# A decoder layer on one core: the order of work of four engines in the loop body, written anew

## The reference, cut to what matters

```python
# x, ctx: (64, 128, 512) float32
x = x + mamba(layernorm(x))                    # inner width 1024, 16 states a channel
x = x + xattn(layernorm(x), ctx)               # 8 heads of 16, tokens 512, band of +-64
x = x + moe(layernorm(x))                      # 8 experts of 16, the best 2 of them

def mamba(x):
    h_in, gate = split(x @ in_proj_w.T)
    u = silu(causal_conv4(h_in) + conv_b)
    ts, Bm, Cm = split(u @ x_proj_w.T)         # 128, 16, 16
    dt = softplus(ts @ dt_proj_w.T + dt_proj_b)
    h[t] = exp(dt[t] * A) * h[t-1] + dt[t] * u[t] * Bm[t]     # for each channel and state
    y = (sum over states of h * Cm + D * u) * silu(gate)
    return y @ out_proj_w.T

def xattn(x, ctx):                             # a sequence is (128 channels, 512 tokens)
    q, k, v = split(x.T @ w_in.T + b_in)
    a = softmax(where(|i - j| <= 64, q k / 4, -inf))
    return w_ct.T @ (relu((a v @ w_out.T + b_out).T) * ctx) + b_ct
```

## Time and profile before

| | |
|---|---|
| median of 3 runs | 5236.79 us (5234.45 to 5239.43) |
| span of the profiled execution | 5221.2 us, 15.6 below the median |
| mean granted TensorE clock | 0.976 |
| one iteration in the loop | 154.7 us |
| share of the span busy | PE 90%, DVE 88%, ACT 84%, POOL 83% |

### The profile page before, as it was taken

The page is one execution under the profiler, slowest core; times in us unless marked ns, Lnnn a source line. Parts: engine busy times, 40 slices in busy tenths (PEclk is TensorE's granted clock), DMA queues, the critical chain, the costliest instruction groups (busy, mean ns, idle before and its releaser), DMA issues. The chain is left out here.

```text
span 5221.2 us, 141020 instructions
## 1 busy us (share of the span) xinstructions
PE 4699.5 (90%) x51012; PEld 3370.9 (65%) x51012; DVE 4617.0 (88%) x6307; ACT 4384.6 (84%) x9314; POOL 4311.4 (83%) x3466
## 2 busy tenths in 40 slices
PE   4789999999999999999999999999999999998976
PEld 3566666666666666666666666666666666666653
DVE  2889999999999999999999999999999999998961
ACT  3788889888898888889988898988889888888862
POOL 2888888888898888888888888888889888888860
PEclk8899999999999999999999999999999999999986
DMA  3202222212222211222221222221222221122200
GB/s 118 74 29 79 70 76 78 78 41 74 72 71 78 78 58 56 72 74 78 74 78 36 78 69 78 78 78 41 73 72 70 78 78 57 57 72 71 66 13 7
DMA packets 114706, 350.31 MB, mean 67 GB/s; under 512 B 13056, under 2 KB 14848, under 8 KB 113920
## 3 DMA queue, kind: packets, MB, share of 16 engines
q1 hardware_dynamic: 114048, 341.51, 20.2%
HBM read 323.64 MB, written 17.83 MB: 65 GB/s over the span
## 5 line engine op out<-in xcount | busy, mean ns | idle before, releaser
L304 POOL TENSOR_TENSOR ring<-du,bc 128x512 f32<-128x512 f32 x2048 | 2594.2, 1284 | 622.0 <-PE ps L1128 408.5
L472 ACT ACTIVATE ps<-delta,a_neg 128x254 f32<-128x254 f32 x4096 | 1767.9, 467 | 38.3 <-DVE ring L1508 25.5
L313 POOL TENSOR_TENSOR ring<-ring,bc 128x512 f32<-128x512 f32 x1280 | 1703.3, 1337 | 109.1 <-DVE ring L1508 106.7
L1508 DVE TENSOR_TENSOR_SCAN ring<-ps,ring 128x512 f32<-128x512 f32 x1280 | 1549.1, 1215 | 102.6 <-ACT ps L472 83.6
L1128 PE MATMUL ps<-ident,ring 128*128 128x128 f32 x8192 | 1096.3, 278 | 46.8 <-POOL ring L313 41.6
L1128 PEld LDWEIGHTS ps<-ident,ring 128*128 128x128 f32 x8192 | 926.1, 142 | 253.2 <-issue 169.7
L1508 DVE TENSOR_TENSOR_SCAN ps<-ps,ring 128x512 f32<-128x512 f32 x768 | 933.6, 1216 | 116.5 <-ACT ps L472 109.7
L1492 DVE TENSOR_TENSOR ring<-ps,bc 128x512 f32<-128x512 f32 x768 | 527.7, 687 | 15.7
L627 ACT ACTIVATE probs_mem<-ps 128x768 f32<-128x768 f32 (+1 forms) x512 | 445.6, 911 | 105.7 <-PE ps L1072 99.5
L1196 PE MATMUL ps<-w_in,xt_a 128*128 128x256 f32 x2048 | 474.3, 386 | 16.1 <-DVE hc L1623 8.1
L1176 PE MATMUL ps<-xt_a,w_in 128*128 128x256 f32 x2048 | 472.0, 384 | 7.6 <-DVE hc L1623 4.1
(11 more groups left out here) (144 smaller groups left out, 6915.0 us busy)
## 6 DMA issues: line engine op xcount, KB each, us to landing
w_in<-in_w_in SPq DMA_DIRECT2D x256, 512.0 KB, 3.7
bc<-bc_rows SPq DMA_DIRECT2D x256, 512.0 KB, 5.1
x_new<-in_x SPq DMA_DIRECT2D x32, 512.0 KB, 7.4
x_res<-in_x SPq DMA_DIRECT2D x32, 512.0 KB, 6.7
enc<-in_ctx SPq DMA_DIRECT2D x64, 256.0 KB, 3.1
out<-x_att SPq DMA_DIRECT2D x32, 512.0 KB, 2.8
w_outp<-in_w_outp SPq DMA_DIRECT2D x1, 2048.0 KB, 8.1
bc_rows<-bc_sb SPq DMA_DIRECT2D x32, 32.0 KB, 1.5
```

Source lines behind the costliest of these rows:

```text
L304: nc.gpsimd.tensor_tensor(ring[:, s % RING, :].rearrange("p (n t) -> p n t", n=2), du[:, q % 2, (ic % 2) * NT:(ic % 2 + 1) * NT].rearrange ...
L313: nc.gpsimd.tensor_tensor(ring[:, s % RING, :], ring[:, s % RING, :], bc[:, s % RS, 2:4, :].rearrange("p a t -> p (a t)"), ALU.mult).then_ ...
L472: nc.scalar.activation(ps[:, s % DAR, (n % 2) * NT:(n % 2 + 1) * NT].rearrange("p (b t) -> p b t", b=GB)[:, :, 1:T], delta[:, ic, :].rearr ...
L1508: nc.vector.tensor_tensor_scan(state, ps[:, s % DAR, :], ring[:, s % RING, :], 0.0, ALU.mult, ALU.add).then_inc(h_done, 1)
```

## The change

In the `iteration` functions of GpSimd, ScalarE, TensorE and VectorE the calls are put in another order. Every engine keeps the same calls, each with its waits, buffers and semaphores; the bodies of the helpers don't change. Some of what moves: on VectorE `shift` e,0 stands ahead of scan 0, and the soft steps of pair 0 stand in a row ahead of scan 62, three of pair 1 in a row behind scan 63; on GpSimd `rstd` e moves behind times_b 2; on ScalarE `soft_exp` 3, `skip_term`s, `attention_x` 1 and the group of `u_silu` and `gate_silu` move; on TensorE the scores s of the attention, h_in, gate_in and y_sum are interleaved otherwise. The diff, cut to the parts that the text speaks of:

```diff
@@ -317,121 +317,122 @@
             def iteration(g, cur, nxt, p1, p2):
                 if cur:
                     times_b(g, 0)
+                    times_b(g, 1)
                 if p1:
                     times_c(g - 1, 62)
+                if cur:
+                    times_b(g, 2)
                 if p2:
                     rstd("e", g - 2, 0, 2)
                 if cur:
-                    times_b(g, 1)
-                    times_b(g, 2)
-                    times_c(g, 0)
                     times_b(g, 3)
                     times_b(g, 4)
                     times_b(g, 5)
+                    times_c(g, 0)
                     times_b(g, 6)
                     times_b(g, 7)
                     times_c(g, 2)
+                    times_b(g, 8)
+                    times_b(g, 9)
...
+                if nxt:
+                    squares("a", g + 1, 0)
+                if p1:
                     variance("t", g - 1, 0)
-                if cur:
-                    soft_exp(g, 2)
-                    decays(g, 8)
-                    decays(g, 9)
...
+                    variance("t", g - 1, 1)
+                if cur:
                     decays(g, 16)
-                if nxt:
-                    x_norm(j, 1)
+                    soft_exp(g, 2)
+                    skip_term(g, 2)
+                if nxt:
+                    x_copy(j, 0)
...
+                    attention_x(g - 1, 1)
+                if cur:
+                    y_back(g, 0)
                     decays(g, 19)
-                    y_back(g, 0)
                     decays(g, 20)
-                    skip_term(g, 3)
+                    soft_exp(g, 3)
                     decays(g, 21)
-                    decays(g, 22)
...
-                if cur:
+                    attention(g, p2, 1, "qk", 3)
+                if cur:
+                    y_back(g, 2)
                     decays(g, 33)
-                    soft_exp(g, 3)
-                    soft_one(g, 3)
-                    skip_term(g, 5)
+                if p1:
...
-                if cur:
-                    decays(g, 44)
+                    skip_term(g, 7)
                 if p1:
                     attention(g, p2, 1, "exp", 0)
-                if cur:
-                    decays(g, 45)
-                    skip_term(g, 7)
-                if p1:
                     attention(g, p2, 1, "exp", 1)
-                    variance("e", g - 1, 0)
                 if cur:
                     decays(g, 46)
                     decays(g, 47)
-                if nxt:
-                    tap3(j, 3)
                 if p1:
                     attention(g, p2, 1, "exp", 2)
                     attention(g, p2, 1, "exp", 3)
+                if nxt:
+                    u_silu(j, 2)
+                if p1:
+                    attention(g, p2, 1, "o", 0)
+                if cur:
+                    y_back(g, 4)
+                if nxt:
+                    gate_silu(j, 0)
+                    u_silu(j, 3)
                 if cur:
                     decays(g, 48)
-                if nxt:
-                    gate_silu(j, 0)
-                if p1:
-                    attention(g, p2, 1, "o", 0)
-                if nxt:
-                    u_silu(j, 2)
-                    u_silu(j, 3)
-                if cur:
-                    y_back(g, 4)
                     decays(g, 49)
                 if p1:
                     attention(g, p2, 1, "exp", 4)
...
-                if nxt:
-                    skip_term(j, 0)
                 if p1:
                     attention(g, p2, 1, "o", 1)
+                if nxt:
+                    step_size(j, 0)
                 if cur:
                     decays(g, 57)
+                if p1:
+                    attention(g, p2, 1, "wide")
+                if nxt:
+                    soft_exp(j, 0)
+                    step_size(j, 1)
+                if cur:
                     decays(g, 58)
-                if p1:
-                    attention(g, p2, 1, "wide")
-                if nxt:
-                    step_size(j, 0)
+                if nxt:
+                    soft_one(j, 0)
                 if cur:
                     decays(g, 59)
                 if nxt:
-                    soft_exp(j, 0)
+                    step_size(j, 2)
...
-                if p2:
                     experts_up(g - 2)
                 if cur:
                     y_sum(g, 9)
+                    y_sum(g, 11)
                 if p1:
                     attention(g, p2, 0, "s", 0)
                 if nxt:
                     transposed_x(g, 0, cur, p1)
+                if cur:
+                    y_sum(g, 13)
                 if p1:
                     attention(g, p2, 0, "s", 1)
-                if cur:
-                    y_sum(g, 11)
-                if p1:
-                    attention(g, p2, 0, "s", 2)
-                if cur:
-                    y_sum(g, 13)
                 if nxt:
                     transposed_x(g, 1, cur, p1)
-                if p1:
-                    attention(g, p2, 0, "s", 3)
                 if cur:
                     y_sum(g, 15)
                     y_turn(g, 0, nxt)
                 if p1:
+                    attention(g, p2, 0, "s", 2)
+                    attention(g, p2, 0, "s", 3)
+                if nxt:
+                    h_in(j, 0, cur)
+                if p1:
                     attention(g, p2, 0, "shift")
-                if nxt:
-                    h_in(j, 0, cur)
-                if p1:
                     attention(g, p2, 0, "st", 0)
...
                 if p1:
                     attention(g, p2, 1, "s", 1)
                 if cur:
                     y_sum(g, 33)
+                    y_sum(g, 35)
+                    y_turn(g, 3, nxt)
+                    y_sum(g, 37)
                 if p1:
                     attention(g, p2, 1, "s", 2)
-                if cur:
-                    y_sum(g, 35)
-                    y_sum(g, 37)
+                if nxt:
+                    gate_in(j, 1, cur)
+                if cur:
+                    y_sum(g, 39)
                 if p1:
                     attention(g, p2, 1, "s", 3)
-                if cur:
-                    y_sum(g, 39)
-                    y_turn(g, 3, nxt)
+                if nxt:
+                    h_in(j, 3, cur)
                 if p1:
                     attention(g, p2, 1, "shift")
-                if nxt:
-                    gate_in(j, 1, cur)
+                if cur:
+                    y_sum(g, 41)
                 if p1:
                     attention(g, p2, 1, "st", 0)
-                if cur:
-                    y_sum(g, 41)
-                if nxt:
-                    h_in(j, 3, cur)
-                if p1:
                     attention(g, p2, 1, "st", 1)
                 if cur:
                     y_sum(g, 43)
                 if p1:
                     attention(g, p2, 1, "av", 0)
...
@@ -1626,57 +1621,58 @@
 
             def iteration(g, cur, nxt, p1, p2):
                 j = g + 1
-                if cur:
-                    scan(g, 0)
                 if p2:
                     shift("e", g - 2, 0)
+                if cur:
+                    scan(g, 0)
+                    soft_step(4, g, 1)
+                if p2:
                     shift("e", g - 2, 1)
-                if p1:
-                    y_step(g - 1, 7)
                 if cur:
                     scan(g, 1)
                     times_c(g, 1)
                     scan(g, 2)
+                if p1:
+                    y_step(g - 1, 7)
+                if cur:
                     scan(g, 3)
                     scan(g, 4)
                     times_c(g, 4)
-                    soft_step(4, g, 1)
                     scan(g, 5)
...
+                if cur:
+                    scan(g, 37)
                     times_c(g, 36)
-                    scan(g, 37)
-                if p1:
-                    attention(g, 1, "max", 0)
-                if cur:
+                    soft_step(2, g, 3)
                     y_step(g, 3)
+                if nxt:
+                    conv(j, 4)
+                    conv(j, 5)
+                if p1:
+                    attention(g, 1, "max", 1)
+                if cur:
                     scan(g, 38)
-                    soft_step(1, g, 3)
-                if p1:
-                    attention(g, 1, "max", 1)
-                if nxt:
...
@@ -1811,40 +1807,37 @@
                     scan(g, 54)
                     scan(g, 55)
                     times_c(g, 55)
+                if p1:
+                    attention(g, 1, "rden")
+                if cur:
                     scan(g, 56)
-                if p1:
-                    attention(g, 1, "rden")
-                if cur:
                     scan(g, 57)
                     times_c(g, 57)
+                if p1:
+                    attention(g, 1, "on")
+                if cur:
                     scan(g, 58)
-                if p1:
```

(20 more changed lines are left out.)

## The result

| | before | changed |
|---|---|---|
| median, us | 5238.1 (4 runs) | 5367.1 (5365.6 to 5370.2, 4 runs) |
| ratio | 1 | 1.0248, 95% interval 1.0234 to 1.0263 |
| span of the profiled execution, us | 5221.2 | 5365.7 |
| VectorE busy, us | 4617.0 | 4783.9 |
| one iteration in the middle, us | 154.7 | 160.4 |

The change makes the kernel 2.5% slower, 129 us. The forecast was 0.4% slower, 5258 us, with a range that ended at 5325.

What follows compares the result with a forecast made beforehand. No engine alone was the bound; VectorE's row of work was taken as the iteration's clock. Waits -2.8 and soft steps +3.5 gave +0.7 us an iteration, 22 us over 31: 5258 us, range 5165 to 5325.

Steps and rivals of the forecast that it cites:

- What costs nothing: Whole program: same instructions, 13 table loads an iteration as before, DMA triggers barely moved, first and last stages at nothing.
- the prediction's own mechanism: A VectorE instruction with two SBUF inputs and a GpSimd instruction reading SBUF contend; the second blocks until the first ends.
- Soft steps, +3.5 us: VectorE's softplus steps, put in rows under a busy GpSimd, take 3.5 us more of VectorE's time an iteration.
- The seven steps at the end: Steps 1 to 4 of pair 0 and 1 to 3 of pair 1: 5.3 and 4.55 us, 2.95 more than before.
- The nine others: The iteration's other soft steps, some newly finding GpSimd idle and some no more: +0.5 us together.
- Waits, 8.5 to 5.7 us: VectorE's waits for other engines over an iteration, summed place by place: a gain of 2.8 us.
- Head of VectorE, 0.5 us: Start of VectorE's iteration: shift e,0 ahead of scan 0 waits 0.5 us for GpSimd's later rstd e.
- (a): Rival: VectorE's soft steps don't pay, as GpSimd is held or idles; only waits count, 5107 to 5150 us; chance 0.30.
- (b): Rival: no net change, waits and soft steps cancel within 0.3 us an iteration, 5227 to 5247 us; chance 0.18.
- (c): Rival: the chain through the attention of sequence 1 becomes the bound, 2.5 us more an iteration, 5335 us; chance 0.10.
- The marks given for a right forecast: End soft steps near 1.8 us, decays' wait 5.5 to about 3, rden over 1 us, rstd e waited for at the head.

Runs made afterwards that it cites:

- after_psum: Changed kernel with the router's exponentials, indices and one comparison mask in PSUM instead of SBUF; 5244.4 us, 1.0010.
- after_tail: Changed kernel with the seven soft steps at the end of VectorE's iteration back where they stood before; 5428.3 us, 1.0375.
- psum_fill01: after_psum with TensorE's scores 2 of sequence 0 ahead of y_sum 15 and y_turn 0, and y_sum 41 between st 0 and st 1 of sequence 1; 5300.2 us, 1.0122.

## Why the prediction was wrong, point by point

- **What costs nothing.** This is the step that failed. It counted table loads and DMA triggers and took the router, whose place on VectorE hardly changes, at nothing, though the prediction's own mechanism applies to it: five instructions with two SBUF inputs beside GpSimd. They cost 3.6 us an iteration, and through the gates 1.6 us of waits and a clock at half for 7 us. after_psum removes exactly this and with it 123 of the 129 us of the whole; of the 5.8 us by which the iteration in the middle grew it takes away 3.4 (157.0 us), and the rest is in the next two terms. The start and the end of the program, also put at nothing, were not nothing either: the first iteration with a scan got 6.6 us shorter and the part behind the last scan 0 4.2.
- **Soft steps, +3.5 us.** The mechanism was right and the size too large: 2.0. The seven steps at the end were put at 5.3 + 4.55 us; the timeline of the changed kernel has 0.97 + 1.65 + 1.66 + 0.69 = 5.0 and 1.13 + 1.64 + 1.64 = 4.4, against 6.9 before. The nine others were to cost 0.5 more and cost 0.5 less. A held step takes 1.64 to 1.66 us rather than the 1.8 assumed: by the traces it ends 0.55 us behind the product that holds it, which is the own pass of 0.56 assumed, so that only 1.1 us of the product were left and not the whole 1.28.
- **Waits, 8.5 to 5.7 us.** They are 9.1. Those forecast came about: 3.1 us at scan 48 (2.7), 1.7 at rden 1 (1.5), 0.4 at addq of sequence 1 (0.6), 0.4 at maximum 0.0 (0.2). On top came 1.6 for the experts, from the router, 0.7 at addq of sequence 0, 1.0 at scan 29 and 0.3 at rden 0, which I had not seen. In after_psum, without the router, the sum is 9.7 in an iteration with two stretches at half clock and 6.9 in one at full clock. So the order does take waits away, 1.6 us of the 2.8 forecast, and this term was mis-sized in two ways: 1.2 us of small waits that I had not seen, and stretches at half clock that the forecast didn't count.
- **Head of VectorE, 0.5 us.** No wait came there. The order it judged risky, rstd e behind times_b, showed its price only in after_tail (3.67 us).
- **Rivals.** (a) is out: the soft steps paid. (b) gives the time that the kernel takes once the router is free, 5244, but not by waits and soft steps that cancel in each iteration: most iterations are 2.3 us longer than before, and a shorter start and end make up for it. (c), 5335 us, came nearest in number, but its cause isn't the one that made the 129 us.
- The marks given for a right forecast (L1479 and L1483 near 1.8 us at the end, the decays' wait down to about 3, over 1 us at rden) appeared in part: 1.65 us, 4.2 us for the decays, and 1.7 at rden; the mark of a wait at the head did not. They marked the terms that had been thought of and couldn't show the one that had not.

## What to carry to other kernels

Where two engines lock each other out, list every instruction that can be held, small ones first: a 16-column instruction of 0.17 us can cost a whole product of 1.2 us of the other engine, and five in a chain cost more than four (5.3 us). Whether they are held is decided by the other engine's pauses and by its short instructions that hold nothing, so ask of a new order which of these it takes away. A run with the cause removed can match the old total by luck: look at one iteration as well. Moving one operand to PSUM took the lock away at no cost, where tensor_scalar didn't.

## What the runs showed of the hardware

A tensor_scalar of 8 columns in SBUF, with its scalars per partition, waits for GpSimd's product as a two-input instruction does (0.95 to 0.97 us against 0.23 to 0.28 free), and so does a copy of 256 columns from SBUF to SBUF (1.28 against 0.29). Beside a product a tensor_reduce of 16 columns (L1579, 0.14), a copy of one column (L1456, 0.15) and a tensor_scalar of one column (L1461, 0.20) were not held, and GpSimd's rstd of 2 columns held no router instruction of the kernel before (L1609 and L1611, 0.175). TensorE's clock was at half for about 7 us behind a wait of 3.65 us. In after_psum it was at half for 3.4 us behind waits of 1.59 and 1.94 us in most iterations and stayed full behind the same waits in two; each iteration with both stretches took 2.8 us longer. In the iteration of psum_fill01 shown it stayed full with waits of 1.70 and 2.30 us at those places.
